# A fused attention and feed-forward kernel: the first hundred microseconds in another order

## The chip, the cores and the metric

The kernel runs on one core of a Trainium2 chip. The metric is the device time of one execution in microseconds (us). The engines are named as in the profile: PE (TensorE, matrix products), DVE (VectorE), ACT (ScalarE), POOL (GpSimd), and SP (SyncE), which here issues every DMA. Each engine takes its own instructions strictly in the order in which the program lists them, and waits at semaphores that the others raise.

## The reference

The input x is 4 batches of 2048 rows of 256 numbers, in fp32. Two layers are applied, each with a residual:

```python
x = x + layernorm(attention(layernorm(x), w_qkv, out_w, out_b))
x = x + layernorm(ffn(layernorm(x), W_r, W_k, W_v, mu_r, mu_k))

# attention: one head of width 256; rows 0-63 and 192-255 of the contraction in fp16, the rest in fp32
q, k, v = split(mixed_precision_matmul(x, w_qkv), 3)
s = softmax(q / sqrt(256) @ k.T)
y = (s @ v) @ out_w.T + out_b

# ffn: x_prev is x shifted by one row in the sequence
xr = mu_r * x + (1 - mu_r) * x_prev;  xk = mu_k * x + (1 - mu_k) * x_prev
out = sigmoid(xr @ W_r.T) * (square(relu(xk @ W_k.T)) @ W_v.T)
```

## The kernel before, in words

**Numbers.** A value that has to be exact beyond fp16 is kept as a high and a low fp16 part, and a product is the sum of three fp16 matmuls. The normed x is stored as three planes of 128 columns (`low`, `high`, and `rest`, which is what `high` leaves over), and DMA transposes turn them into `turned`. Two weight pairs are multiplied together once at the start: the query and key weights into one matrix `qk` (QK_BANK), and the value and output weights into one (FOLD_BANK). So the kernel needs only "queries" = x times `qk`, scores = queries times x, values = probabilities times x, and one projection.

**Tiling.** A batch is 4 groups of 512 rows for preparation (`n` in `pre_stats_of(n)`, `planes_low(n)`, `turn_planes(n)`; group 0 in two halves) and 8 units of 256 rows for queries (`h`, H = 32 in all). A unit has 8 score blocks of 128 x 512; block k = 8h + u is five matmuls of 512 columns into one of three PSUM banks (`scores(k)`, L1457 to L1461), and DVE copies it out and takes its maximum (`score_out(k)`, L1134). Block k waits until DVE has copied out block k - 3. In unit 0, blocks 0 and 1 read group 0 of `turned`, blocks 2 and 3 group 1, blocks 4 and 5 group 2, blocks 6 and 7 group 3.

**Slots.** Every engine has a loop over slots k = 0 ... 255. In slot k PE does score block k and then what is due there; the other engines do their shares of the units underway. The constants at the head of the file (L88 to L99 and those above) say in which slot something is due: `at(k, X)` is unit h if k = 8h + X. So queries of unit h are made in slot 8h - 6 by PE, rounded (q_hi) in slot 8h - 5 by ACT and their low part (q_lo) in slot 8h - 3 by DVE; score block 8h waits for it.

**The head.** Before the loop come, by hand, the load and rounding of the query and key weights, their transposes (L1554) and product (L1566), the scale of it (largest element, summed over partitions by the matmul L1586, `weight_factors`), then the parts of group 0, `queries(0)`, and for groups 1 to 3 the chain

- DVE `pre_stats_of` (L1010) and `pre_moments_of` (L1016), the row statistics;
- POOL `pre_rsqrt` (L513, L518), their inverse roots;
- DVE `pre_norm` (L1022);
- ACT `planes_high` (L752), POOL `planes_low` (L674), the three planes;
- SP `turn_planes` (L386), the transpose.

Between them PE runs matmuls on a constant tile whose result is not used (`keep_clock`, L1572; WARM gives their counts at four places). At the end of slot 1 PE transposes the value and output weights (`turn_weight(2)`, `(3)`), makes `queries(1)` and multiplies the two weights (`multiply_weights(2, 3, ...)`); in slot 7 it transposes the other three. Then the scales of these weights are found: peaks on DVE (slots 1 and 8), a transpose and a spreading matmul on PE (slots 15 and 19), `diagonal_of_peaks` and `tops` on DVE (slots 17 and 20), `scales` on POOL (one slot later), and the weights are rounded in two pairs by ACT (slots 24 and 27) and DVE (25 and 28). The softmax of unit 0 is spread over slots 7 to 14 (exponentials and high parts on ACT, low parts on POOL and DVE), and its values begin on PE in slot 23.

Of the kernel before, what the change touches and what calls it, by code (L numbers as in the profile page):

```python
# [18 lines left out]
def sandwich(nc, x, w_qkv, out_w, out_b, w_r, w_k, w_v, mu_r, mu_k, out):  # L19
# [3 lines left out]
    NJ = N // BLK  # L23
# [67 lines left out]
    NORM_AT = 0  # L91
    V_AT = 1
    WEIGHT_PEAKS_AT = 1
    FIRST_LOW = 2
    WARM = (22, 8, 28, 16)
    PREP, PREP_EVERY = 23, 11
    PREP_LOAD, PREP_STATS, PREP_RSQRT, PREP_NORM, PREP_HIGH, PREP_LOWER, PREP_TURN = -8, 0, 1, 2, 4, 5, 6
    WEIGHTS_AT, VAL_AT, PEAKS_AT, PEAKS_TURN_AT, DIAGONAL_AT, SPREAD_AT, TOPS_AT = 7, 9, 8, 15, 17, 19, 20
    W_HIGH_AT, W_LOW_AT = (24, 27), (25, 28)  # L99
# [11 lines left out]
    with ctx:  # L111
# [250 lines left out]
        def _(sp):  # L362
# [79 lines left out]
            load_weight(3)  # L442
            for i, m in enumerate((mu_r, mu_k)):
                for h in range(HALVES):
                    sp.dma_start(mu[:, i, h:h + 1], m[h * P:(h + 1) * P].rearrange("(p a) -> p a", a=1)).then_inc(vec_in, 16)
            turn_planes(1)
# [3 lines left out]
            reload_x(NJ)  # L450
            reload_x(NJ + 1)
            for k in range(SLOTS):
# [8 lines left out]
                if (n := prep(k, PREP_LOAD)) is not None and n >= NJ + 2:  # L461
                    reload_x(n)
# [26 lines left out]
        def _(pool):  # L489
# [190 lines left out]
            pre_rsqrt(2)  # L680
            pre_rsqrt(3)
            planes_low(1)
# [67 lines left out]
        def _(act):  # L750
# [166 lines left out]
            query_high(1)  # L917
            row_norms_of()
            for k in range(SLOTS):
# [21 lines left out]
                if (h := at(k, Q_HIGH)) is not None and h >= 2:  # L941
                    query_high(h)
# [6 lines left out]
                if k == VAL_AT:  # L949
                    keep_val()  # L950
# [56 lines left out]
        def _(dve):  # L1007
# [282 lines left out]
            dve.wait_ge(x_in[1], 16)  # L1290
            stats_of(1, range(1))
# [3 lines left out]
            stats_of(1, range(1, 2))  # L1295
            weight_factors()
            half_low(1)
            stats_of(1, half(1))
            qk_low()
            pre_moments_of(1)  # L1300
            pre_stats_of(2)
            pre_moments_of(2)
            query_low(0)
            pre_norm(1)
            pre_stats_of(3)
            pre_moments_of(3)
            pre_norm(2)
            dve.wait_ge(kappa_made, 2)
            for k in range(SLOTS):
                score_out(k)  # L1310
                if k == NORM_AT:
# [5 lines left out]
                if (h := at(k, Q_LOW)) is not None and h >= 1:  # L1317
                    query_low(h)
# [9 lines left out]
                for i in range(2):  # L1328
                    if (h := at(k, MIX[i])) is not None:
                        mix(h, i)  # L1330
                if (h := at(k, INVERT)) is not None:
# [88 lines left out]
        def _(pe):  # L1420
# [170 lines left out]
            for k in range(SLOTS):  # L1591
# [10 lines left out]
                if (h := at(k, FEED)) is not None:  # L1602
                    feed(h)
                if k == V_AT:
# [3 lines left out]
                    pe.wait_ge(q_lo_made, 1)  # L1608
                    queries(1)
                    multiply_weights(2, 3, FOLD_BANK, out_multiplied)  # L1610
                if (h := at(k, QUERY)) is not None and h >= 2:
                    pe.wait_ge(q_lo_made, h)
                    queries(h)
# [73 lines left out]
```

## Time and profile before

| | us |
|---|---|
| median of 3 runs | 810.1 (809.94 to 810.55) |
| the profiled execution, its own time | 810.1 |
| its span in the trace | 808.3 |
| PE busy | 783.5 (97%) |
| DVE busy | 655.2 (81%) |
| ACT busy | 574.8 (71%) |
| POOL busy | 516.0 (64%) |

The span runs from the first to the last record; 1.8 us of the execution lie outside it. Of the chain of waits that ended last, PE holds 91%. A busy share is an average over the whole span, so the stage that the change touches, the first 60 us, has to be read in the timelines of the engines, one beside the other.

### The profile page before, as it was taken

To read this page: it belongs to the slowest core of one execution; us is meant where nothing else is said; L and a number is where in the kernel's file an instruction comes from. 1 tells how busy PE (TensorE), PEld (TensorE's weight loads), DVE (VectorE), ACT (ScalarE), POOL (GpSimd) and SP (SyncE) were. 2 spreads that over 40 slices of the span, in tenths; PEclk is the share of its full clock that TensorE was granted. 3 is DMA by queue.
4 is the path that set the end of the run, shared out by engine and by line. 5 is a ranking of instruction groups with operands and counts; after the bars stand their busy time and mean duration, and the time that the engine had idled before them with its cause. 6 is when DMAs were issued, how large, how long until landed. Compare 5 with 4: busy or idle time off the path is not lost.

```text
span 808.3 us, 16563 instructions
## 1 busy us (share of the span) xinstructions
PE 783.5 (97%) x5839; PEld 573.9 (71%) x5839; DVE 655.2 (81%) x1685; ACT 574.8 (71%) x791; POOL 516.0 (64%) x750
## 2 busy tenths in 40 slices
PE   8899999999999999999999999999999999998983
PEld 6547767777777777777777777777777777777862
DVE  6788888877788979878788879988777788777886
ACT  3568668877677778777768687787777776675564
POOL 2351356656766868775676767876567657676674
PEclk9999999999999999999999999999999999999999
DMA  6787788577867769787767887857577765559201
GB/s 188 151 162 129 147 152 179 90 143 145 169 130 147 137 131 168 144 148 135 111 133 139 172 164 142 158 103 136 108 139 144 131 125 91 120 119 206 74 14 52
DMA packets 348243, 108.70 MB, mean 134 GB/s; under 512 B 321920, under 2 KB 347904, under 8 KB 348160
## 3 DMA queue, kind: packets, MB, share of 16 engines
q1 hardware_dynamic: 348160, 107.64, 69.0%
q8 instruction: 46, 0.75, 0.4%
q14 instruction: 37, 0.30, 0.1%
HBM read 18.75 MB, written 8.39 MB: 34 GB/s over the span
## 4 chain that ended last, share of the span: by engine, by line
PE 91%; DVE 4%; DMA 2%; issue 1%; POOL 1%; ACT 1%; SPq 0%; POOLq 0%; DVEq 0%; ACTq 0%
PE Y L1478 7%; PE Y L1482 7%; PE Y L1481 7%; PE Y L1479 7%; PE Y L1480 7%; PE S L1457 7%; PE S L1461 7%; PE S L1460 7%; PE S L1459 7%; PE S L1458 7%; PE M L1422 6%; PE M L1424 6%; PE M L1423 6%; PE M L1437 1%; PE M L1440 1%
## 5 line engine op out<-in xcount | busy, mean ns | idle before, releaser
L1134 DVE TENSOR_SCALAR_CACHE_REDUCE probs<-S 128x512 f32<-128x512 f32 x256 | 172.9, 677 | 63.5 <-PE S L1461 63.3
L820 ACT ACTIVATE probs<-probs,exp_bias,kappa 128x2048 f32<-128x2048 f32 x64 | 133.9, 2092 | 63.6 <-DVE exp_bias L1147 63.6
L1152 DVE TENSOR_TENSOR p_lo<-probs,p_hi 128x2048 f16<-128x2048 f32 x62 | 170.1, 2743 | 7.2 <-ACT p_hi L752 7.1
L1479 PE MATMUL Y<-pt_lo,planes 128*128 128x256 f16 x496 | 135.2, 273 | 0.0
L1481 PE MATMUL Y<-pt_lo,planes 128*128 128x256 f16 x496 | 135.2, 273 | 0.0
L1478 PE MATMUL Y<-pt_hi,planes 128*128 128x256 f16 x496 | 135.2, 273 | 0.0
L1480 PE MATMUL Y<-pt_hi,planes 128*128 128x256 f16 x496 | 135.2, 273 | 0.0
L1482 PE MATMUL Y<-pt_hi,planes 128*128 128x256 f16 x496 | 135.2, 273 | 0.0
L752 ACT ACTIVATE p_hi<-probs 128x2048 f16<-128x2048 f32 x64 | 121.4, 1896 | 5.3 <-DMA pt_lo<-p_lo 5.0
L1457 PE MATMUL S<-turned,q_hi 128*128 128x512 f16 x256 | 97.1, 379 | 2.4 <-DMA turned<-planes 1.4
L1461 PE MATMUL S<-turned,q_lo 128*128 128x512 f16 x256 | 97.0, 379 | 0.0
L1459 PE MATMUL S<-turned,q_hi 128*128 128x512 f16 x256 | 97.0, 379 | 0.0
L1460 PE MATMUL S<-turned,q_hi 128*128 128x512 f16 x256 | 97.0, 379 | 0.0
L1458 PE MATMUL S<-turned,q_lo 128*128 128x512 f16 x256 | 97.0, 379 | 0.0
L569 POOL TENSOR_TENSOR avar<-amv,att_eps 128x2 f32<-128x2 f32 x32 | 8.9, 278 | 116.3 <-DVE amv L1184 116.3
L665 POOL TENSOR_TENSOR gate<-gate,res 128x256 f32<-128x256 f32 x54 | 82.5, 1547 | 0.9 <-ACT gate L902 0.9
L651 POOL TENSOR_TENSOR xm_lo<-mixed,xm_hi 128x512 f16<-128x512 f32 x61 | 77.8, 1277 | 6.2 <-ACT xm_hi L752 5.9
L1479 PEld LDWEIGHTS Y<-pt_lo,planes 128*128 128x128 f16 x496 | 48.5, 98 | 30.5
L1478 PEld LDWEIGHTS Y<-pt_hi,planes 128*128 128x128 f16 x496 | 48.5, 98 | 30.5
L1209 DVE SCALAR_TENSOR_TENSOR mixed<-diff,mu,xt 128x256 f32<-128x256 f32 x128 | 64.2, 542 | 1.5 <-POOL diff L644 1.2
L601 POOL TENSOR_TENSOR gvar<-gmv,gate_eps 128x2 f32<-128x2 f32 x32 | 6.8, 212 | 86.2 <-DVE gmv L1229 86.1
L1171 DVE SCALAR_TENSOR_TENSOR att<-M,inv_sum,bias_row 128x256 f32<-128x256 f32 x64 | 28.0, 478 | 37.5 <-PE M L1424 35.9
(223 smaller groups left out, 2031.7 us busy)
## 6 DMA issues: line engine op xcount, KB each, us to landing
x_res<-in_L_attn_x SPq DMA_DIRECT2D x32, 256.0 KB, 3.7
out_x<-gate SPq DMA_DIRECT2D x32, 256.0 KB, 3.2
xs<-in_L_attn_x SPq DMA_DIRECT2D x13, 512.0 KB, 4.6
pt_hi<-p_hi SPq DMA_TRANSPOSE x62, 5.0
pt_lo<-p_lo SPq DMA_TRANSPOSE x62, 4.8
xs<-in_L_attn_x SPq DMA_DIRECT2D x2, 256.0 KB, 4.3
gate<-in_L_attn_x SPq DMA_DIRECT2D x1, 512.0 KB, 6.9
att<-in_L_attn_x SPq DMA_DIRECT2D x1, 512.0 KB, 4.3
```

Source lines behind the costliest of these rows:

```text
L1134: dve.tensor_scalar(probs[:, h % 2, t, c * BLK:(c + 1) * BLK], S[k % RING][:, :], 1.0, None, ALU.mult, ALU.max, accum_out=chunk_max[:, t, ...
L1152: dve.tensor_tensor(p_lo[:, t, :], probs[:, h % 2, t, :], p_hi[:, t, :], ALU.subtract).then_inc(p_lo_made, 1)
L1457: pe.matmul(to, q_hi[:, h % 2, 0, rows], low, start=True, stop=False)
L1458: pe.matmul(to, q_lo[:, h % 2, 0, rows], low, start=False, stop=False)
L1459: pe.matmul(to, q_hi[:, h % 2, 1, rows], high, start=False, stop=False)
L1460: pe.matmul(to, q_hi[:, h % 2, 1, rows], rest, start=False, stop=False)
L1461: pe.matmul(to, q_lo[:, h % 2, 1, rows], high, start=False, stop=True).then_inc(s_done, 1)
L1478: pe.matmul(to[:, 0, :], low, p_h, start=first, stop=False, skip_group_check=True)
L1479: pe.matmul(to[:, 0, :], low, p_l, start=False, stop=final, skip_group_check=True)
L1480: pe.matmul(to[:, 1, :], high, p_h, start=False, stop=False, skip_group_check=True)
L1481: pe.matmul(to[:, 1, :], high, p_l, start=False, stop=False, skip_group_check=True)
L1482: mm = pe.matmul(to[:, 1, :], rest, p_h, start=False, stop=final, skip_group_check=True)
```

## The change

What it does, engine by engine:

- **SP:** the transpose of group 1 is issued ahead of four small loads (mu), not behind them. The loads of x for groups 4 and 5 move from before the loop to slots 15 and 26.
- **POOL:** `planes_low(1)` stands ahead of `pre_rsqrt(3)`, not behind it.
- **ACT:** `query_high(1)` moves into slot 3, and the row norms of a weight (`row_norms_of`) move from before the loop to slot 6, with `keep_val` (from slot 9).
- **DVE:** the statistics of the first two tiles of group 1 move behind `half_low(1)` (they stood one by one in front of `weight_scale` and `weight_factors`). `query_low(0)` moves behind `pre_norm(1)`, and the moments of group 2 behind that. `pre_norm(2)` and the moments of group 3 move into slot 0, `pre_norm(3)` into slot 1, the peaks of three weights from slot 1 to slot 4. In every slot `query_low` stands behind `probs_low`, `attention`, the statistics and `mix`, not ahead of them.
- **PE:** `queries(1)` moves from slot 1 to slot 2, and the product of the value and output weights from slot 1 to slot 3; the other three transposes from slot 7 to slot 5. The unused matmuls are 22, 18, 18, 12, not 22, 8, 28, 16.
- The search for the scales and the rounding of the weights move from slots 15 ... 28 to slots 11 ... 20.

```diff
-    NORM_AT = 0
+    NORMS_AT = (0, 1)
     V_AT = 1
-    WEIGHT_PEAKS_AT = 1
+    WEIGHT_PEAKS_AT = 4
-    WARM = (22, 8, 28, 16)
+    WARM = (22, 18, 18, 12)
-    WEIGHTS_AT, VAL_AT, PEAKS_AT, PEAKS_TURN_AT, DIAGONAL_AT, SPREAD_AT, TOPS_AT = 7, 9, 8, 15, 17, 19, 20
-    W_HIGH_AT, W_LOW_AT = (24, 27), (25, 28)
+    FOLD_AT, WEIGHTS_AT, VAL_AT, PEAKS_AT, PEAKS_TURN_AT, DIAGONAL_AT, SPREAD_AT, TOPS_AT = 3, 5, 6, 8, 11, 12, 15, 16
+    W_HIGH_AT, W_LOW_AT = (17, 19), (18, 20)
@@ SP
             load_weight(3)
+            turn_planes(1)
             for i, m in enumerate((mu_r, mu_k)):
...
-            turn_planes(1)
             turn_planes(2)
             turn_planes(3)
             sp.dma_start(bias_row[:, :], ...)
-            reload_x(NJ)
-            reload_x(NJ + 1)
...
-                if (n := prep(k, PREP_LOAD)) is not None and n >= NJ + 2:
+                if (n := prep(k, PREP_LOAD)) is not None:
                     reload_x(n)
@@ POOL
             pre_rsqrt(2)
+            planes_low(1)
             pre_rsqrt(3)
-            planes_low(1)
             planes_low(2)
@@ ACT
             planes_high(3)
-            query_high(1)
-            row_norms_of()
...
-                if (h := at(k, Q_HIGH)) is not None and h >= 2:
+                if (h := at(k, Q_HIGH)) is not None and h >= 1:
                     query_high(h)
...
                 if k == VAL_AT:
+                    row_norms_of()
                     keep_val()
@@ DVE
             half_norm(0)
-            dve.wait_ge(x_in[1], 16)
-            stats_of(1, range(1))
             weight_scale()
             half_low(0)
             half_norm(1)
-            stats_of(1, range(1, 2))
             weight_factors()
             half_low(1)
+            dve.wait_ge(x_in[1], 16)
+            stats_of(1, half(0))
+            qk_low()
             stats_of(1, half(1))
-            qk_low()
             pre_moments_of(1)
             pre_stats_of(2)
+            pre_norm(1)
+            query_low(0)
             pre_moments_of(2)
-            query_low(0)
-            pre_norm(1)
             pre_stats_of(3)
-            pre_moments_of(3)
-            pre_norm(2)
             dve.wait_ge(kappa_made, 2)
             for k in range(SLOTS):
                 score_out(k)
-                if k == NORM_AT:
+                if k == NORMS_AT[0]:
+                    pre_norm(2)
+                    pre_moments_of(3)
+                if k == NORMS_AT[1]:
                     pre_norm(3)
...
-                if (h := at(k, Q_LOW)) is not None and h >= 1:
-                    query_low(h)
                 if (ht := exp_at(k, FIRST_LOWER, LOWER)) is not None and (ht[1] > 0 or ht[0] >= FIRST_LOW):
                     probs_low(*ht)
...
                         mix(h, i)
+                if (h := at(k, Q_LOW)) is not None and h >= 1:
+                    query_low(h)
@@ PE
+                if (h := at(k, QUERY)) is not None and h >= 1:
+                    pe.wait_ge(q_lo_made, h)
+                    queries(h)
                 if k == V_AT:
                     pe.wait_ge(w_rounded, 2)
                     turn_weight(2)
                     turn_weight(3)
-                    pe.wait_ge(q_lo_made, 1)
-                    queries(1)
+                if k == FOLD_AT:
                     multiply_weights(2, 3, FOLD_BANK, out_multiplied)
-                if (h := at(k, QUERY)) is not None and h >= 2:
-                    pe.wait_ge(q_lo_made, h)
-                    queries(h)
```

## Rows read from the trace of the kernel before

**Rows 1.** Page, part 1: busy us, share of the span, instructions per engine.
```profile
PE 783.5 (97%) x5839; PEld 573.9 (71%) x5839; DVE 655.2 (81%) x1685; ACT 574.8 (71%) x791; POOL 516.0 (64%) x750
```

**Rows 2.** Windows: length, busy us (instructions) per engine, clock, DMA share, GB/s.
```profile
17.90:26.77 8.87, 6.50 (x36) 4.12 (x37) 8.72 (x23) 6.00 (x13) 4.30 (x6) 1.00 0.75 187
...
45.27:57.00 11.73, 10.74 (x60) 5.55 (x59) 9.90 (x32) 8.45 (x7) 5.32 (x5) 1.00 0.76 143
57.00:120.00 63.00, 63.00 (x451) 44.03 (x452) 54.33 (x144) 41.71 (x53) 24.31 (x50) 1.00 0.80 146
```

**Rows 3.** Timeline of PE: start, us, what, [idle before <- releaser].
```profile
11.00 0.38 PE L1586 MATMUL M<-w_peak,twos 128*128 128x1 f32 x2
...
17.90 0.38 PE L1457 MATMUL S<-turned,q_hi 128*128 128x512 f16 x1 [0.38 <-DMA turned<-planes]
...
21.31 0.65 PE L1554 MATMUL Y<-ident,pt_hi 128*128 128x128 f32 x4 [1.09 <-ACT pt_hi L752]
...
23.74 1.99 PE L1566 MATMUL M<-res 128*128 128x256 f32 x8 [0.24 <-ACT res L752]
26.77 0.39 PE L1457 MATMUL S<-turned,q_hi 128*128 128x512 f16 x1 [1.04 <-DMA turned<-planes]
...
27.86 0.38 PE L1457 MATMUL S<-turned,q_hi 128*128 128x512 f16 x1
...
37.81 0.27 PE L1437 MATMUL M<-turned,qk_hi 128*128 128x256 f16 x1
...
38.90 0.38 PE L1457 MATMUL S<-turned,q_hi 128*128 128x512 f16 x1
...
46.50 0.39 PE L1457 MATMUL S<-turned,q_hi 128*128 128x512 f16 x1 [0.86 <-DVE probs L1134]
```

**Rows 4.** Timeline of DVE.
```profile
12.18 0.14 DVE L1074 TENSOR_SCALAR w_sum<-M 128x1 f32<-128x1 f32 x1
...
14.37 0.37 DVE L1016 BATCH_NORM_AGGREGATE pmv<-pst 128x2 f32<-128x6 f32 x4
14.66 1.37 DVE L1010 BATCH_NORM_STATS2 pst<-gate 128x6 f32<-128x256 f32 x4
...
16.47 0.66 DVE L1125 SCALAR_TENSOR_TENSOR q_lo<-M,q_hi 128x512 f16<-128x512 f32 x1
17.05 1.37 DVE L1022 TENSOR_SCALAR xs<-xs,pmv,prstd 128x256 f32<-128x256 f32 x4
...
43.55 2.28 DVE L1152 TENSOR_TENSOR p_lo<-probs,p_hi 128x2048 f16<-128x2048 f32 x1
...
53.77 1.93 DVE L1120 TENSOR_SCALAR weight_scale_of<-inv_top 128x4 f32<-128x4 f32 x1
```

**Rows 5.** Timeline of POOL.
```profile
15.10 1.01 POOL L518 TENSOR_TENSOR prstd<-pvar,minus_half 128x4 f32<-128x4 f32 x1
...
21.72 1.16 POOL L674 TENSOR_TENSOR planes<-xs,planes 128x512 f16<-128x512 f32 x1
...
51.60 4.08 POOL L670 TENSOR_TENSOR p_lo<-probs,p_hi 128x2048 f16<-128x2048 f32 x1 [9.62 <-ACT p_hi L752]
```

**Rows 6.** Timeline of ACT.
```profile
18.46 1.15 ACT L752 ACTIVATE planes<-xs 128x512 f16<-128x512 f32 x2 [2.05 <-DVE xs L1022]
...
60.81 2.10 ACT L820 ACTIVATE probs<-probs,exp_bias,kappa 128x2048 f32<-128x2048 f32 x1 [4.59 <-DVE exp_bias L1147]
...
62.90 0.67 ACT L777 ACTIVATE wt_hi<-Y,weight_scale_of 128x512 f16<-128x512 f32 x1
```

**Rows 7.** Chain that ended last: start, us, what; the transpose before score block 2.
```profile
22.90 3.82 DMA turned<-planes
```

**Rows 8.** Timeline of PE near the end.
```profile
739.35 0.28 PE L1422 MATMUL M<-wt_hi,xm_hi 128*128 128x256 f16 x1 [2.60 <-POOL xm_lo L651]
```

**Rows 9.** Windows of PE there: length, busy us (matmuls), clock, DMA share, GB/s.
```profile
740.00:741.00 1.00, 1.00 (x7) 0.50 1.21 208
...
743.00:744.00 1.00, 1.00 (x10) 0.81 1.16 220
```

## The prediction

> **What bounds the kernel.** The first part of the page comes first: PE is busy for 783.5 of the 808.3 us [rows 1]. So it is not a question of how much the other engines do but of where PE stands still, and the second view is the windows. After 57 us PE has no idle time (63.00 of 63.00 us [rows 2]), and nothing that the change touches lies later than slot 28, so the head decides. There PE is idle for 2.37 us between 17.90 and 26.77, and for 0.99 us between 45.27 and 57.00 [rows 2]. The timeline of PE names the places: block 0 waits for a transpose until 17.90, the weight transposes wait for ACT until 21.31, block 2 waits 1.04 us for the transpose of group 1 until 26.77, and the block at 46.50 waits 0.86 us for DVE [rows 3]. The point to see is that the wait before 26.77 is what is left after PE has filled the time with useful work: the two weight transposes, `queries(1)` and the weight product (1.99 us, from 23.74 [rows 3]) all lie before it. The third view is the chain and the timelines of DVE, POOL and ACT, which show what makes the transpose of group 1 late.
>
> **The change, first stretch: up to block 2.** I follow the new order on DVE with the old durations.
>
> 1. The scale of `qk`. The peak matmul now follows 18 unused matmuls, not 8. The ten extra ones cost about 0.11 us each (a 256-column fp16 matmul: the ten of `queries` take 38.90 - 37.81 = 1.09 us [rows 3]), so it moves from 11.00 to 12.1, and with its 0.38 us DVE can go on at 12.5, not at 12.18 [rows 3, 4]: +0.3 us.
> 2. Two of the four statistics of group 1 used to run in front of such waits. They are now in the open: half of 1.37 us less overlap, +0.66 [rows 4]. With 0.1 for a drain that `qk_low` covered, the moments of group 1 move from 14.37 to 15.5.
> 3. The statistics of group 2 follow at 15.8 (before: 14.66) and end at 17.1. POOL's inverse roots came 0.73 + 1.01 us behind the start of the moments (16.11 against 14.37 [rows 4, 5]), so now at 17.25. `pre_norm(1)` runs 17.3 to 18.6. It was at 17.05, so ACT's planes of group 1 (18.46 [rows 6]) hardly move: 18.6 to 19.75.
> 4. `query_low(0)` now waits in line behind `pre_norm(1)`: 18.6 to 19.3, where it started at 16.47 [rows 4]. Block 0 needs it. It starts at 19.3, not at 17.90 [rows 3]. Blocks 0 and 1 and the weight transposes are done by 22.4 instead of 22.2, so this alone costs little.
> 5. The moments of group 2 run behind it, 19.2 to 19.6. POOL makes the roots of group 2 (another 1.35 us with its gaps) before `planes_low(1)`, which starts at 21.05 instead of 21.72 and takes 1.16 [rows 5]. SP is free: the four small loads are behind the transpose now. The transpose is issued at 22.25, not at 22.90, and lands after the same 3.82 us [rows 7], at 26.1. The two edits aimed at the transpose therefore bring 0.65 us; the rest of what they could bring is eaten by steps 1 to 4.
>
> So block 2 starts at 26.1, 0.65 us earlier. But `queries(1)` (1.09 us) and the product (1.99 us alone, 1.85 in a stream) have moved behind it, and PE has nothing to do from 22.4 to 26.1. Sum: -0.65 + 1.09 + 1.85 = **+2.3 us**. Nothing later gives this back, since PE was never idle between 26.77 and 45. The transposes of groups 2 and 3 are late too, and are hidden: `pre_norm(2)` at 21.5 puts group 2 on its way at about 26.4 and group 3 at about 30.2. They land by 30.3 and 34.1, and PE comes to blocks 4 and 6 at 31.2 and 34.6 (blocks of 1.09 us [rows 3], the other three weight transposes included). The margin of the second is 0.5 us. The loads of x moved to slots 15 and 26 are first read from slot 23 on, so they are free.
>
> **The clock.** Half rate is seen in this trace where PE had stood idle for 2.60 us before 739.35 [rows 8]: the granted clock is 0.50 (1.2 GHz) in the next windows, 7 matmuls in 1 us, and on its way back to full (2.4 GHz) at 743 [rows 9]. About 3.4 us at half rate lost 1.7 us. The gaps of 1.09 and 1.04 us in the head lost nothing. The new gap, 3.7 us, is longer than 2.60, and another of almost 2 us (from the end of the 12 unused matmuls to 19.3) stands before it. The fall is the likelier outcome. Its price lies between 0 (no fall, or all of it inside the gap) and 1.7 us; part of the slow stretch may lie in the gap, and I take **+1.2 us**. The Trainium skill, TensorE: Matmul & The Clock Gate, section "HAM oscillation — how this bites in real kernels", says that a wait for a DMA between two bursts of matmuls makes the engine go back to half rate. By that rule the fall is certain here and the sum includes it; rows 8 and 9 agree with the rule, the 1 us gaps set it a lower bound.
>
> **Second stretch: slots 8 to 28.** Old: the stall of 0.86 us at 46.50, because DVE makes a low part of 2.28 us (43.55 [rows 4]) in front of two copies. New: in slot 13 `query_low(2)` stands behind that low part, and block 16 needs it. From the end of block 13: copy 0.6, low part 2.2, `query_low` 0.65, with two hand-overs 3.55 us, against 2.0 for blocks 14 and 15. Block 16 was not held before; block 17 was: 46.50 is 4.2 us after block 13's end (the low part starts 1.25 us behind that end). It now starts at 3.55 + 1.09 = 4.65: +0.45. The spreading matmul (about 0.4 with its gap) moves into this stall: -0.4. The transpose of the peaks (0.11) leaves it: +0.1. In `tops` a 128x4 operation takes 1.93 us and ends exactly with POOL's low part (51.60 + 4.08 = 55.68) [rows 4, 5]; in slot 16 POOL is idle, which takes away the rest of the old idle time, -0.1 to -0.3. Against it, ACT gets four weight roundings of 0.6 us (62.90) in slots 17 and 19, where before they stood behind a 4.59 us gap (60.81) [rows 6]. They push exponentials and the high part of slot 21 back by 2.5 us, and the low part on DVE in slot 22 behind them; block 26 would wait 0.6. Sum +0.4; the bounds are -0.9 (all idle time of this stretch gone) and +1.5 (both new waits in full, no credit). I take **+0.4 us**.
>
> `query_low` behind `mix` in later units: slot 8h - 3 holds neither `probs_low` nor `mix` from unit 3 on (their slots are 3 and 6, 0 and 2 modulo 8), so there the order is the same.
>
> **Sum.** 2.3 + 1.2 + 0.4 = 3.9 us. The profiled execution has a span of 808.3 us and a time of 810.1, which is the median of the runs, so the forecast is 812.2 in the span and **814.0 us** as time.
>
> **The rivals.**
>
> - *No fall of the clock.* Everything as above, but the slow stretch does not come. For it: gaps of 1 us cost nothing. Against: the 2.60 us gap did [rows 8, 9]. 814.0 - 1.2 = 812.8.
> - *Later still.* The transposes of groups 2 and 3 eat their margin, for DVE's norms run beside POOL's low parts and SP has four loads between transposes 1 and 2. If group 3 lands 1.5 us later than I say, block 6 waits 1.0; with the full 1.7 for the clock, 815.5.
> - *Not slower: the transpose comes as early as its inputs allow.* The place is `planes_low(1)`. If it starts right behind ACT's planes (19.75) and not behind POOL's roots of group 2, the transpose is issued at 20.95 and lands at 24.8: -1.97 + 2.94 = +0.97. The gap is then near 2.3 us and the clock holds. If the second stretch also loses its whole 0.99 us of idle time and gains a little beside, the end is 0.0: 810.1, 809.5 at best. It decides at the issue of that transpose, at about 21 us. Against it: POOL's order has `pre_rsqrt(2)` ahead, and DVE gives it its moments only behind `query_low(0)`.
> - *The delay on DVE does not come* (block 0 starts near 18 because the added overlap loss is smaller than I count), while `queries(1)` and the product still cost 2.94: the transpose about 1 us earlier, no fall: 811.4. For it: my step 2 rests on waits that were partly cover. Against: the order of `query_low(0)` is plain in the program.
>
> **How the numbers follow.** Chances: forecast 0.48, no fall 0.22, later still 0.08, not slower 0.09, no delay on DVE 0.13. A measurement of this kernel can tell about 0.2%, 1.6 us, from no change: 808.5 to 811.7. The forecast and the first two rivals lie above that, 0.78; I take 0.03 from "no fall" for a low end of its second stretch and add 0.04 of the last rival, whose 811.4 is close to the bound: slower 0.79. Within lie the other 0.09 of the last rival, that 0.03, and 0.03 of "not slower": 0.15. The other 0.06 of "not slower" I give to faster, for a case in which the second stretch brings more than its idle time. The range goes from the last rival with a little room, 811.0, to the second with a little room, 815.6.
>
> **What would show it.** In the new trace: block 0 starts near 19.3, released by q_lo; PE idle for more than 3 us before block 2, which starts near 26 and is released by `turned`; `queries(1)` and the product behind it; block 8 starts about 2.3 us later than before where the clock is full; a window of clock 0.50 within 30 us; block 16 released by q_lo in slot 16. Wrong would be: block 2 before 25, block 0 at 18, or PE idle again removed later, after 57 us, where I see none to remove.

## The result, and the profile after

The changed kernel is slower: 814.76 us in the median of 4 runs (814.14 to 815.58) against 810.02 us; the ratio is 1.0060, 95% interval 1.0043 to 1.0079. The forecast was 814.0. The profiled execution has a span of 814.2 us and a time of its own of 815.95, which is 1.2 us above the median; its stages are read below, and they add up to more than the medians differ.

The first line of the page: PE does the same work in a longer span [rows 1].

```profile
PE 784.2 (96%) x5835; PEld 574.4 (71%) x5835; DVE 655.9 (81%) x1685; ACT 574.8 (71%) x791; POOL 512.9 (63%) x750
```

The timeline of PE with the places where it waits (start, us, what, [idle before <- releaser]). The row of 25.55 stands where 26.77 stood before, 49.56 in the neighbourhood of 46.50 [rows 3].

```profile
18.84 0.39 PE L1454 MATMUL S<-turned,q_hi 128*128 128x512 f16 x1 [2.00 <-DVE q_lo L1122]
...
25.55 0.61 PE L1454 MATMUL S<-turned,q_hi 128*128 128x512 f16 x1 [3.50 <-DMA turned<-planes]
...
27.65 0.42 PE L1434 MATMUL M<-turned,qk_hi 128*128 128x256 f16 x1
...
30.11 1.89 PE L1563 MATMUL M<-res 128*128 128x256 f32 x8
31.84 0.38 PE L1454 MATMUL S<-turned,q_hi 128*128 128x512 f16 x1
...
37.47 0.38 PE L1454 MATMUL S<-turned,q_hi 128*128 128x512 f16 x1
...
49.56 0.39 PE L1454 MATMUL S<-turned,q_hi 128*128 128x512 f16 x1 [1.79 <-DVE q_lo L1122]
...
62.63 0.39 PE L1454 MATMUL S<-turned,q_hi 128*128 128x512 f16 x1 [2.07 <-DVE q_lo L1122]
```

Three things are to be seen. The waits have moved: 2.00 us before block 0 (0.38 before the change), 3.50 before block 2, and two new ones for q_lo, 1.79 before block 16 and 2.07 before block 24. The queries (27.65) and the product (30.11) now stand behind block 2. And the first matmuls of block 2 are longer than 0.39 us.

The windows of PE around that place (length, busy us and matmuls, granted clock, DMA share, GB/s):

```profile
24.00:26.00 2.00, 0.45 (x2) 0.71 0.48 73
26.00:28.00 2.00, 2.00 (x7) 0.50 0.70 120
28.00:30.00 2.00, 2.00 (x15) 0.94 0.42 77
```

The clock falls to 0.50 (1.2 GHz) between 24 and 26 us, inside the gap, and comes back between 28 and 30.

DVE and POOL in the same stretch:

```profile
15.01 0.38 DVE L1013 BATCH_NORM_AGGREGATE pmv<-pst 128x2 f32<-128x6 f32 x4
...
16.80 1.38 DVE L1019 TENSOR_SCALAR xs<-xs,pmv,prstd 128x256 f32<-128x256 f32 x4
18.10 0.68 DVE L1122 SCALAR_TENSOR_TENSOR q_lo<-M,q_hi 128x512 f16<-128x512 f32 x1
...
45.19 0.91 DVE L1107 TENSOR_SCALAR peak_diag<-ident,peak_of 7x7 f32<-7x7 f32 x1
...
57.44 0.75 DVE L1087 SCALAR_TENSOR_TENSOR wt_lo<-M,weight_scale_of,wt_hi 128x512 f16<-128x512 f32 x1 [0.37 <-ACT wt_hi L775]
58.10 3.25 DVE L1087 SCALAR_TENSOR_TENSOR wt_lo<-relu,weight_scale_of,wt_hi 128x512 f16<-128x512 f32 x1
...
61.89 0.08 DVE L1131 DVE_READ_ACCUMULATOR probs<-S 128x1 f32 x1
```

```profile
20.41 1.16 POOL L672 TENSOR_TENSOR planes<-xs,planes 128x512 f16<-128x512 f32 x1
...
41.99 4.09 POOL L668 TENSOR_TENSOR p_lo<-probs,p_hi 128x2048 f16<-128x2048 f32 x1 [12.99 <-ACT p_hi L750]
...
56.73 4.08 POOL L668 TENSOR_TENSOR p_lo<-probs,p_hi 128x2048 f16<-128x2048 f32 x1
```

SP issues the transpose of group 1 at 21.59 and not at 22.90 [rows 7], and it lands 3.9 us later:

```profile
21.59 1.45 SPq L386 DMA_TRANSPOSE turned<-planes  x1
```

Where the time went, by the start of a score block in the two profiled executions (the last column names what was added or gained since the row above):

| start of | before | after | difference | what added |
|---|---|---|---|---|
| block 2 | 26.77 | 25.55 | -1.2 | earlier transpose |
| block 8 | 34.57 | 37.47 | +2.9 | product and queries +2.8, half rate +1.3 |
| block 17 | 46.50 | 50.65 | +4.15 | order of q_lo and a held operation +0.65, a later q_hi from ACT +0.6 |
| block 24 | 56.97 | 62.63 | +5.7 | a held rounding: +1.5 |
| block 28 | 66.75 | 72.41 | +5.7 | |
| end | 808.3 | 814.2 | +5.9 | |

Nothing is added between blocks 24 and 28, and 0.2 us in all that follows. In this pair of executions the whole loss is made in 63 us. The parts of block 17's row, and what "held" means, follow with the experiments.

### The profile page after: what moved, and what is told of

It reads as the page before. It is cut to its first block, busy times and chain, and to the rows that moved or that the text cites. A ratio compares the mean times of both kernels' runs of the same rounds, so it can differ in the third digit from the quotient of the medians.

```text
span 814.2 us, 16555 instructions
## 1 busy us (share of the span) xinstructions
PE 784.2 (96%) x5835; PEld 574.4 (71%) x5835; DVE 655.9 (81%) x1685; ACT 574.8 (71%) x791; POOL 512.9 (63%) x750
## 4 chain that ended last, share of the span: by engine, by line
PE 90%; DVE 4%; DMA 2%; issue 1%; ACT 1%; POOL 1%; SPq 0%; POOLq 0%; DVEq 0%; ACTq 0%
PE Y L1475 7%; PE Y L1479 7%; PE Y L1477 7%; PE Y L1478 7%; PE Y L1476 7%; PE S L1454 6%; PE S L1458 6%; PE S L1455 6%; PE S L1457 6%; PE S L1456 6%; PE M L1419 6%; PE M L1421 6%; PE M L1420 6%; PE M L1434 1%; PE M L1435 1%
## 5 line engine op out<-in xcount | busy, mean ns | idle before, releaser
L567 POOL TENSOR_TENSOR avar<-amv,att_eps 128x2 f32<-128x2 f32 x32 | 6.8, 211 | 116.3 <-DVE amv L1181 116.3
```

## The experiments

Each is given with its edit, what was expected before it ran, and what came. Times are medians. The kernel before was run again beside each of three groups of experiments, with 810.03, 810.12 and 810.08 us. Where a start of a block or a length of a stretch is given, it is that of the one profiled execution.

### The order of query_low in the slots undone

```diff
+                if (h := at(k, Q_LOW)) is not None and h >= 1:
+                    query_low(h)
                 if (ht := exp_at(k, FIRST_LOWER, LOWER)) is not None and (...):
                     probs_low(*ht)
...
-                if (h := at(k, Q_LOW)) is not None and h >= 1:
-                    query_low(h)
```

> The changed kernel with query_low ahead of probs_low in each slot of DVE, as before the change. Theory: block 16 no longer waits for q_lo at the far side of the 2.3 us low part (1.79 us of wait); block 17 then waits for its bank as in the kernel before (about 1.2 us), so block 17 starts 0.5 us earlier. Whether the end follows depends on the wait at block 24: if that is set by POOL's low part (fixed by ACT and the scales, which also move up by 0.5), the end is 0.5 us earlier, 814.3. Rival: the order costs the whole 1.79 us and the kernel is 1.8 us faster, 813.0.

Measured: 814.77 us (812.95 to 816.9), ratio to before 1.0060 (1.0039 to 1.0081); the median is that of the changed kernel. The timeline of PE:

```profile
51.24 0.39 PE L1454 MATMUL S<-turned,q_hi 128*128 128x512 f16 x1 [1.20 <-DVE probs L1131]
...
63.73 0.49 PE L1454 MATMUL S<-turned,q_hi 128*128 128x512 f16 x1 [2.57 <-DVE q_lo L1122]
```

The wait before block 16 is gone, and block 17 waits 1.20 us for its bank instead. From block 8 to block 17 this kernel takes 12.7 us (38.55 to 51.24) and the changed one 13.2: the half microsecond of the theory. It did not reach the end: the wait before block 24 grew from 2.07 to 2.57, because POOL's low part (57.8 to 61.9 here) did not move against block 8. These rows refute the rival; the times alone, which scatter over 4 us, would not. The profiled execution is the slowest of the four (816.9): its clock was at 0.50 once more from 63.9 to 67.3, behind that wait, where the changed kernel kept 1.00.

### The second rounding of weights two slots later

```diff
-    W_HIGH_AT, W_LOW_AT = (17, 19), (18, 20)
+    W_HIGH_AT, W_LOW_AT = (17, 19), (18, 22)
```

> The changed kernel with the second pair of low weight parts on DVE in slot 22 (behind the low part of the probabilities there), not in slot 20. The same work, at a time when POOL's low part (56.7 to 60.8) is over. Theory 'lock' (the DVE operation of 3.25 us was held by POOL's operation on the same memory port): both roundings take 0.75 us, block 24 no longer waits for q_lo (2.07 us before), and the kernel is 1.5 to 2.1 us faster, about 813.0. Rival 'load' (DVE simply has 1.4 us more to do in these slots): the rounding takes 3 us here too or another operation does, block 26 waits instead, and the gain is under 0.5 us.

Measured: 813.87 us (812.82 to 814.3), ratio 1.0043 (1.0027 to 1.0060), 0.9 us better than the changed kernel. DVE and PE in this kernel:

```profile
64.05 0.74 DVE L1087 SCALAR_TENSOR_TENSOR wt_lo<-relu,weight_scale_of,wt_hi 128x512 f16<-128x512 f32 x1
```

```profile
65.45 0.39 PE L1454 MATMUL S<-turned,q_hi 128*128 128x512 f16 x1 [1.30 <-DVE probs L1131]
```

The rounding of the last weight takes 0.74 us here and took 3.25 in the changed kernel, with the same operands. Block 24 no longer waits, so the mechanism "lock" holds. Of the "load" rival the duration is refuted, but the wait of block 26 that it named is there: it waits for a copy that stands behind the low part on DVE (61.18 to 63.47) and behind the two roundings themselves, 1.3 us of work in their new slot. So only part of the 2.07 us came through; from block 17 to block 28 it takes 21.0 us, not 21.8. The size of 1.5 to 2.1 was wrong, measured 0.9.

### The whole second stretch as before the change

```diff
-    ... PEAKS_TURN_AT, DIAGONAL_AT, SPREAD_AT, TOPS_AT = ..., 11, 12, 15, 16
-    W_HIGH_AT, W_LOW_AT = (17, 19), (18, 20)
+    ... PEAKS_TURN_AT, DIAGONAL_AT, SPREAD_AT, TOPS_AT = ..., 15, 17, 19, 20
+    W_HIGH_AT, W_LOW_AT = (24, 27), (25, 28)
     (and query_low ahead of probs_low, as above)
```

> The changed kernel with the second stretch of the kernel before: query_low ahead of probs_low, and the search for the scales and the rounding of the weights in slots 15 to 20 and 24 to 28. What is left of the change is the first stretch. Theory: block 8 stays 2.9 us late (1.6 for the moved queries and product less the earlier transpose, 1.3 for the clock), the waits at blocks 16 and 24 shrink to the 0.9 us of the kernel before, and the kernel is 2.5 to 2.8 us faster than the changed one and 2.0 to 2.9 slower than before: about 812.2. Rival (the second stretch hides lateness of the first): it comes back to within 1 us of the kernel before.

Measured: 812.27 us (810.96 to 812.99), ratio 1.0027 (1.0015 to 1.0039). Its PE rows:

```profile
25.24 0.48 PE L1454 MATMUL S<-turned,q_hi 128*128 128x512 f16 x1 [3.29 <-DMA turned<-planes]
...
50.07 0.39 PE L1454 MATMUL S<-turned,q_hi 128*128 128x512 f16 x1 [1.46 <-DVE probs L1131]
```

By the medians, undoing the second stretch gives back 2.5 of the 4.7 us and leaves 2.2. The rows divide otherwise. Block 8 is 3.0 us later than before (37.53) and block 28 3.6 us later (70.33). From block 8 to block 28 the kernel before takes 32.18 us, the changed one 34.94 and this one 32.80: 2.1 us are undone and 0.6 are left. That this execution still ends only 1.9 us behind the kernel before comes from the clock near the end. At the wait of 2.6 us there, where the clock of the kernel before fell [rows 8, 9], it did not fall here, and from block 28 to the end this kernel takes 739.9 us and not 741.6:

```profile
743.00:745.00 2.00, 2.00 (x20) 1.00 1.15 219
```

So the agreement with the expected 812.2 is partly luck. The 0.6 us that are left lie before block 17 (1.46 us of waiting, before the change 0.86). They come from ACT. The first exponential of unit 0 started 0.87 us before block 8 and now starts 0.32 us after it, for the other three weight transposes, which stood between blocks 7 and 8, stand in slot 5 now, and block 8 follows block 7 at once. Then q_hi is late and DVE waits for it. The first row is from the kernel before, the other two are from this one:

```profile
33.70 2.09 ACT L820 ACTIVATE probs<-probs,exp_bias,kappa 128x2048 f32<-128x2048 f32 x1 [6.40 <-DVE exp_bias L1147]
...
37.85 2.09 ACT L818 ACTIVATE probs<-probs,exp_bias,kappa 128x2048 f32<-128x2048 f32 x1 [1.68 <-DVE exp_bias L1144]
...
46.52 0.69 DVE L1122 SCALAR_TENSOR_TENSOR q_lo<-M,q_hi 128x512 f16<-128x512 f32 x1 [0.52 <-ACT q_hi L750]
```

No run moved these transposes alone; all nine profiled kernels that have them in slot 5 start this exponential 0.3 us after block 8, and all five that have them in slot 7 start it 0.9 to 1.0 us before.

### The moved queries and product alone, in the kernel before

```diff
                     turn_weight(3)
-                    pe.wait_ge(q_lo_made, 1)
-                    queries(1)
+                if k == 3:
                     multiply_weights(2, 3, FOLD_BANK, out_multiplied)
-                if (h := at(k, QUERY)) is not None and h >= 2:
+                if (h := at(k, QUERY)) is not None and h >= 1:
```

> The kernel before with one part of the change: on PE the queries of unit 1 in slot 2 and the product of the value and output weights in slot 3, both behind the wait for the transpose of group 1 and no longer in front of it. Theory 'fill': block 2 starts at 26.8 as before, PE is idle for over 4 us in front of it, block 8 is 1.1 + 1.75 = 2.8 us later plus about 1.3 for the half-rate stretch: 3 to 4 us slower than before, 813 to 814.2. Rival: later waits absorb it, under 1 us.

Measured: 815.15 us (813.08 to 815.92), ratio 1.0061 (1.0044 to 1.0078). This one part costs as much as the whole change. Its row of block 2 in the timeline of PE, and the windows behind it:

```profile
27.13 0.39 PE L1457 MATMUL S<-turned,q_hi 128*128 128x512 f16 x1 [4.20 <-DMA turned<-planes]
```

```profile
28.00:30.00 2.00, 2.00 (x10) 0.50 0.78 146
30.00:32.00 2.00, 2.00 (x9) 0.66 0.68 135
```

The gap is 4.20 us, the clock falls behind its end, and block 8 starts at 39.42, 4.85 us later than before: 0.36 from a later start of the stretch, 2.8 the moved work and 1.7 the half rate.

### The gap before block 2 filled

```diff
                     turn_weight(3)
+                    keep_clock(32)
```

> The changed kernel with 32 unused 256-column matmuls on PE behind the weight transposes of slot 1, so that PE is busy (about 3.5 us) until the transpose of group 1 lands. Theory 'clock' (the gap before block 2 costs its own length, and besides it a stretch at half rate worth 1.3 us): block 2 starts where it did (about 25.5), the granted clock stays at 1.00 between 24 and 30 us, and the kernel is 1.3 us faster than the changed kernel, about 813.4. Rival 'phase' (the half-rate stretch would have come at this place anyway or its cost is absorbed by later waits): within 0.3 us of the changed kernel, 814.8.

Measured: 818.52 us (818.02 to 819.35), ratio 1.0106: 3.8 us slower than the changed kernel, against both theories. The windows of PE show a first reason; a row of DVE and one of POOL are shown for the lock:

```profile
20.00:22.00 2.00, 2.00 (x6) 0.50 0.65 211
22.00:24.00 2.00, 2.00 (x14) 0.68 0.65 123
```

```profile
59.50 2.28 DVE L1087 SCALAR_TENSOR_TENSOR wt_lo<-relu,weight_scale_of,wt_hi 128x512 f16<-128x512 f32 x1
```

```profile
57.14 4.09 POOL L668 TENSOR_TENSOR p_lo<-probs,p_hi 128x2048 f16<-128x2048 f32 x1
```

The half rate came at 20 us, behind the 2.00 us gap before block 0, and the filling itself ran in it, so that block 2 starts at 27.13 and not at 25.55. A second half-rate stretch lies at 50.6 to 54.0 us. Up to block 28 (72.84) only 0.4 us are lost against the changed kernel; 1.5 more come near the end, with a wait that the next experiment shows. The profiled execution (818.02) is the fastest of the four, so that the rest of the 3.8 us is not in this trace. (The rounding on DVE takes 2.28 us here, not 3.25: it began later beside a POOL operation that ends at 61.23, and ended 0.55 after it.)

### Both gaps filled

```diff
-    WARM = (22, 18, 18, 12)
+    WARM = (22, 18, 18, 28)
...
                     turn_weight(3)
+                    keep_clock(28)
```

> The changed kernel with unused matmuls in both gaps of the first stretch: 28, not 12, behind queries(0) (the gap of 2.0 us before block 0) and 28 behind the weight transposes of slot 1 (the gap of 3.5 us before block 2). The first try filled the second gap alone, and the half-rate stretch then began in the first, under the filling. Theory 'clock': with both filled, the clock is 1.00 from the start to block 16, blocks 0 and 2 start where they did, block 8 is 1.3 us earlier than in the profiled execution of the changed kernel, and the median falls by the price times the share of executions in which the clock fell, about 1 us: 813.8. Rival: filling costs as much as it saves (block 2 is pushed back): 814.8 or more.

Measured: 816.80 us (815.47 to 817.32), ratio 1.0086. In the head it went as the theory says:

```profile
19.36 0.39 PE L1454 MATMUL S<-turned,q_hi 128*128 128x512 f16 x1 [0.26 <-DVE q_lo L1122]
...
25.90 0.39 PE L1454 MATMUL S<-turned,q_hi 128*128 128x512 f16 x1 [0.21 <-DMA turned<-planes]
...
746.55 0.28 PE L1419 MATMUL M<-wt_hi,xm_hi 128*128 128x256 f16 x1 [3.42 <-POOL xm_lo L649]
```

The waits are 0.26 and 0.21 us, the clock is 1.00 until block 24, and blocks 2 to 8 take 10.61 us, not 11.92. The end is nevertheless 2 us later than without filling (in the profiled executions 1.4). Two parts are to be seen. First, the clock fell behind the wait of 2.07 us before block 24, at 61.7 to 65.1, where the changed kernel had the same wait and kept 1.00: blocks 24 to 28 take 11.46 us, not 9.78. So the saving of 1.3 us before block 8 is lost again 25 us later. Second, near the end PE waits 3.42 us for POOL's xm_lo, where the kernel before waits 2.60 [rows 8] and the changed one 2.61. In all four kernels with added unused matmuls this wait is 3.4 to 4.5 us; in the ten other profiled executions of this case it is 2.6.

In the chain that leads to that wait ACT's high part waits for the landing of a transpose of a low part. The first row is from the changed kernel, the second from this one; the last is this one's DMA queue of instruction loads in the window 735.5 to 736.5 us (packets, MB, share of 16 engines):

```profile
732.98 5.09 DMA pt_lo<-p_lo
...
733.66 5.94 DMA pt_lo<-p_lo
...
q8 instruction: 1, 0.02, 5.5%
```

This transpose takes 5.1 to 5.2 us in the ten executions and 5.9 to 7.0 in the four, and the wait grows by just as much in each. In the four a load of 16 KB of instructions falls into its flight, in the ten none does: there the load comes after the landing, in the flight of the next such transpose, which takes 5.6 to 5.9 us there and 4.4 in the four. This queue loads once for about every 254 of PE's matmuls and weight loads (46 times for twice 5835), so matmuls added in the head move every later load against the work. Over all 14 traces the transposes of high and low parts of probabilities take 5.7 us in the median with one of these loads in their first 4 us (352 of them) and 4.8 without (1384). No run moved a load alone, so this is what fits all 14 traces, not what an experiment has shown.

### The same filling with the second stretch of before

```diff
     (the second stretch as before the change, and:)
+    WARM = (22, 18, 18, 28)
+                    keep_clock(28)
```

> The changed kernel with the second stretch of the kernel before (query_low in front, scales and weight rounding in slots 15 to 28) and with both gaps filled as in the run above. If lateness is the sum of three terms (moved queries and product less the earlier transpose 1.6 us; half rate about 1; second stretch 2.5), only the first is left: 1.2 to 1.8 us slower than before, 811.6. Rival: there is a further term that I have not seen, and it stays above 812.3.

Measured: 813.31 us (812.44 to 815.14), ratio 1.0050 (1.0036 to 1.0063), 1 us slower than without the filling. Block 28 starts at 69.21, 2.5 us after the kernel before, 1.1 us earlier than unfilled; the wait near the end is 3.6 us, 1.0 longer, and behind it the clock fell (743.3 to 746.8), where the unfilled execution kept it. The rival is right: there were further terms, these two, and the 0.6 us of the later q_hi.

### The moved work alone, with its gap filled

```diff
     (queries(1) and the product moved, in the kernel before, and in their place:)
                     turn_weight(3)
+                    keep_clock(34)
```

> The kernel before with queries(1) and the product moved behind the wait for the transpose of group 1, as in the run that moved only these two, and with 34 unused matmuls where they were. PE does as much as in that run, with no gap in front of block 2. Theory: the clock holds, and what is left is the bare length of the moved work, 2.8 us: 812.9, and 2 us faster than the run without the filling. Rival: the length of the moved work was not the price, and it stays at 815.

Measured: 815.28 us (814.69 to 815.84), ratio 1.0069. The head again does what was said: block 8 at 37.21, 2.6 us later than before, where the kernel without the filling was 4.85 later. The time does not follow: the wait near the end is 4.45 us, 1.85 longer than before. So the head supports "fill", and the time alone would refute it.

### query_low(0) ahead of pre_norm(1)

```diff
             pre_stats_of(2)
-            pre_norm(1)
             query_low(0)
+            pre_norm(1)
```

> The changed kernel with query_low(0) ahead of pre_norm(1). Theory: block 0 starts 1.3 us earlier (near 17.6), but block 2 still waits for the transpose of group 1, so PE only waits at another place: within 0.4 us of the changed kernel, apart from the clock. Rival (the late block 0 is on the path): 1.3 us faster, 813.4.

Measured: 817.51 us (816.46 to 817.86), ratio 1.0095.

```profile
17.58 0.38 PE L1454 MATMUL S<-turned,q_hi 128*128 128x512 f16 x1 [0.78 <-DMA turned<-planes]
...
25.09 0.55 PE L1454 MATMUL S<-turned,q_hi 128*128 128x512 f16 x1 [3.48 <-DMA turned<-planes]
```

Block 0 starts 1.3 us earlier, as said, and block 2 still waits 3.48 us for the same transpose. So the late block 0 is not on the path, and the rival is refuted. That the median is 2.7 us higher was not expected. In the profile block 8 is where it was (37.38), but a second half-rate stretch (62 to 66 us, behind the 2.07 us wait) makes blocks 24 to 28 1.6 us later. The profiled execution (816.46) shows that, and it is the fastest of the four; the other three were not profiled, so that the rest of the 2.7 us stays open.

### The low plane of group 1 still earlier on POOL

```diff
             pre_rsqrt(1)
-            pre_rsqrt(2)
             planes_low(1)
+            pre_rsqrt(2)
             pre_rsqrt(3)
```

> The changed kernel with the low plane of group 1 ahead of the roots of group 2 too. It is the point from which my rival 'not slower' was to decide. Theory: the low plane starts at 19.3, the transpose is issued at 20.5 and lands at 24.4, block 2 starts 1.1 us earlier; the gap before it shrinks to 2.4 us, and if the clock then holds, 1.3 more: 1.1 to 2.4 us faster, 812.4 to 813.7. Rival: group 2 is late by 0.9 us and takes it back, 814.7.

Measured: 815.89 us (815.21 to 818.48), ratio 1.0080 (1.0061 to 1.0098), 1.1 us slower by the medians, with an interval that overlaps that of the changed kernel: no gain, where 1.1 to 2.4 us were expected. SP and PE:

```profile
21.07 1.76 SPq L386 DMA_TRANSPOSE turned<-planes  x1
...
19.28 0.39 PE L1454 MATMUL S<-turned,q_hi 128*128 128x512 f16 x1 [2.00 <-DVE q_lo L1122]
...
26.10 0.39 PE L1454 MATMUL S<-turned,q_hi 128*128 128x512 f16 x1 [1.93 <-DMA turned<-planes]
```

The transpose is issued 1.0 us earlier against its stage (21.07; the stage starts 0.44 later here), but it lands 5.0 us after its issue, not 3.9 as in the changed kernel, so block 2 gains nothing. The last of the four weight loads was issued at 18.98, 2.1 us before it; in the changed kernel it was 3.9 us before. The clock fell behind the 2.0 us gap at 19.28, again behind 26.10, and a third time at 51.3. This was the point from which the rival "not slower" was to decide. In this execution the earlier issue is lost in the later landing. Why it lands later no run tells; the last weight load lands at 23.4 here and at 23.3 in the changed kernel, in the middle of the transpose in both.

### The same idea in the kernel before

```diff
-            pre_rsqrt(3)
             planes_low(1)
+            pre_rsqrt(3)
```

> The kernel before with one part of the change: on POOL the low plane of group 1 ahead of the roots of group 3. Theory: its transpose is issued at 21.4 (when SP has issued the four small loads) and not at 22.9, lands at 25.2, and the 1.04 us of idle time before block 2 disappear, since PE is busy until 25.7 anyway: 1.0 us faster, 809.0. Rival 'next in line': group 2 or 3 is late instead, gain under 0.3.

Measured: 809.57 us (808.24 to 810.18, 11 runs), ratio 0.9992 (0.9983 to 1.0000).

```profile
24.03 1.99 PE L1566 MATMUL M<-res 128*128 128x256 f32 x8 [1.10 <-ACT res L752]
...
30.73 0.39 PE L1457 MATMUL S<-turned,q_hi 128*128 128x512 f16 x1 [0.26 <-DMA turned<-planes]
```

Block 2 starts at 25.86 with no wait, 0.9 us earlier. Half of it is given back: the product waits 1.10 us for ACT and block 6 waits 0.26 for its transpose; block 28 is 0.35 us earlier. The gain is half of what was expected, 0.55 us of 1.0, and the interval of the ratio just reaches 1.

### That, and the low part of unit 0 a slot later

```diff
     (planes_low(1) ahead of pre_rsqrt(3), as above, and:)
-    FIRST_LOWER = (10, 13)
+    FIRST_LOWER = (10, 14)
```

> The kernel before with the low plane of group 1 ahead of the roots of group 3 on POOL (measured alone: 0.5 us faster), and the low part of the second half of unit 0 on DVE one slot later (14, not 13), so that block 17 does not wait for a copy behind it. Theory: the 0.86 us wait before block 17 goes, block 18 waits 0.4 instead: 0.4 us faster than the first edit alone, 809.1. Rival: the wait moves on in full, 809.6.

Measured: 809.91 us (808.88 to 812.31, 11 runs), ratio 1.0004 (0.9995 to 1.0012): no faster than before.

```profile
53.22 2.41 DVE L1120 TENSOR_SCALAR weight_scale_of<-inv_top 128x4 f32<-128x4 f32 x1
...
51.52 4.08 POOL L670 TENSOR_TENSOR p_lo<-probs,p_hi 128x2048 f16<-128x2048 f32 x1 [9.75 <-ACT p_hi L752]
...
47.03 0.39 PE L1457 MATMUL S<-turned,q_hi 128*128 128x512 f16 x1 [0.39 <-DVE probs L1134]
...
56.90 0.39 PE L1457 MATMUL S<-turned,q_hi 128*128 128x512 f16 x1 [0.62 <-DVE q_lo L1125]
```

Block 17 starts at 45.40, 0.74 us earlier than with the first edit alone, and the wait before block 18 is the 0.39 foreseen. The 809.1 that was expected did not come, nor did the first edit's gain. It is lost again: in slot 20 an operation on 4 numbers per row waits 2.41 us for POOL's low part (51.52 + 4.08 = 55.60; 53.22 + 2.41 = 55.63), q_lo is late and block 24 waits. No version beats the kernel before clearly.

## Why the prediction was right

Three terms were summed: 2.3 us for the first stretch, 1.2 for the clock, 0.4 for the second. The profiled execution has 1.6, 1.3 and 2.8, and 0.2 after that, 5.9 in all. The first term was 0.7 too large, the third 2.4 too small, and the median lies 1.2 us under the profiled execution. The mechanism of the first two is right; that the forecast came within 0.8 us of the median is in part luck.

**First stretch, steps 1 to 5.** Right in order and cause. The moments of group 1 ran at 15.01 (said: 15.5), `pre_norm(1)` at 16.80 (17.3), block 0 at 18.84 (19.3), the transpose was issued at 21.59 (22.25) and block 2 started at 25.55 (26.1), 3.50 us of waiting (3.7). All times are some 0.5 us too late in my account, 0.3 us of it because this execution reached the product of `qk` earlier (7.90 against 8.22), the rest from step 1. The stretch without the clock came to +1.6, or +1.9 without that head start, not +2.3. The experiments confirm what sets it: block 2 waits for the transpose whatever happens to block 0, and the moved 2.8 us are the price.

**The clock.** Right in size where it happens. Blocks 2 to 8 take 11.9 to 12.3 us in six profiled kernels in which the clock fell there (the changed kernel and those with the order undone, the old second stretch, the moved work alone, query_low(0) first, the low plane earlier) and 10.6 in the others with this order of work: 1.3 to 1.7 us. It does not always happen. The kernel with the later rounding had the same gap, 3.48 us, and kept 1.00; the kernel with the low plane earlier fell behind gaps of 2.0. The Trainium skill, TensorE: Matmul & The Clock Gate, section "HAM oscillation — how this bites in real kernels", says that such a wait between bursts brings the engine back to half rate. These traces agree at six of the seven unfilled gaps before block 2 and not at that one. The prediction counted the fall as certain by the rule and likely by the rows; the rows were the better guide, and they were weaker than the prediction took them. The wait of 2.6 us near the end, on which they rest [rows 8, 9], stands in ten profiled executions, and the clock fell there in five of them: from block 28 to the end those take 741.6 to 741.7 us and the others 739.9 to 740.9.

**Second stretch.** The mechanism was half right and the size wrong: +0.4 was said (the terms listed there add up to 0.45 to 0.65), +2.8 measured between blocks 8 and 28 of the profile; undoing the stretch took 2.1 of it away there, and 2.5 us off the median. Block 16 waited for q_lo behind the low part, as said. What failed first is the step that costed operations at their free duration in their new slots. I had seen one operation of DVE end exactly with POOL's low part [rows 4, 5], and booked only the relief. The new slots put two others under the same fate. `peak_diag` (7 numbers a row) ran 0.91 us beside the low part of 41.99 + 4.09 = 46.08, where it took 0.22 before (row below); with the old order of q_lo it is worth at most 0.15 us (the kernel with the order undone takes 12.7 us from block 8 to 17, the one with the whole old second stretch 12.54). The rounding from relu at 58.10 ran 3.25 us and ended 0.54 after 56.73 + 4.08 = 60.81. In five more kernels it ended 0.54 or 0.55 after POOL as well, with durations of 2.2 to 3.27 us. The rounding just before it, of the same size but from PSUM (57.44), took 0.75 beside the same operation. So it is the rounding with both its tensors in SBUF that is held.

```profile
48.95 0.22 DVE L1110 TENSOR_SCALAR peak_diag<-ident,peak_of 7x7 f32<-7x7 f32 x1
```

The Trainium skill, SBUF — State Buffer, section "Who interferes with whom", states it: a DVE instruction with two SBUF inputs contends with a GpSimd instruction that reads SBUF. One with at most one such input does not, outside the modes in which DVE uses two ports for one tensor; `tensor_scalar` can enter these. For the two roundings these traces agree, with 3.25 and 0.75 us. `peak_diag` and the 128x4 operation are `tensor_scalar` with one tensor in SBUF and were held too; whether they ran in such a mode no view shows.

The second step that failed is one that the prediction does not have: it moved the three weight transposes to slot 5 and put the effect on ACT at nothing. It is the +0.6 us of the later q_hi.

**ACT's four roundings.** Said to delay block 26 by 0.6. In the changed kernel it does not wait. With the rounding two slots later DVE waits 2.67 us for ACT's high part and starts its low part 1.5 us into block 24, where the others start it 0.5 us in: the delay by ACT is there. The 1.3 us that block 26 waits are not its price, for the two roundings on DVE, 1.3 us of work, stand there in front of the same copy. What ACT's delay costs alone is not shown.

**The rivals.** "No fall" is what the profiled execution with the later rounding did before block 2; the profiled one of the changed kernel fell, and its other runs were not profiled. "Not slower" was tried at its own point and failed on the landing of the transpose. "The delay on DVE does not come" is refuted: block 0 started at 18.84, released by q_lo (and its 811.4 should have been 811.8, 814.0 less 1.2 for the clock and 1 for the transpose). "Later still" (transposes of groups 2 and 3) did not occur: blocks 4 and 6 never waited. After 57 us nothing of the old idle time was there to be removed, but the second stretch added to it up to block 24.

**What stays open.** The median (+4.7) is 1.2 us less than the profiled difference; the profiled execution is the slowest of the five, and the places where the clock falls vary between executions. How the other four divide is not known. That an instruction load is what lengthens the wait near the end fits every trace but was not tried by itself.

## What to carry to other kernels

Work that stands in front of a wait is free up to the length of that wait; before moving it behind, read what is left of the wait: 2.8 us of matmuls moved behind a transfer that came 1.2 us earlier cost more than they could bring, and left a gap in which the clock could fall. An operation has its short duration only in the slot where it was measured: before moving it, look at what POOL does in the new slot if it is one of DVE. Filling a gap for the clock's sake has to be judged by the whole time, since here it won up to 1.7 us at its place and the kernels ended 0 to 4 us later: the next wait let the clock fall instead, and more instructions on PE moved the loads of its program into other transfers. And a median of some executions is not the sum of one trace: list where the clock was low in both traces before dividing a difference among causes.

## What the runs showed of the hardware

- A 7x7 operation of DVE took 0.91 us and a 128x4 one 2.41 us beside a 4.08 us operation of POOL, each ending within 0.03 us of it; without it they took 0.22 and 0.17.
- A 128x512 rounding of DVE with both tensors in SBUF took 2.2 to 3.3 us beside such an operation and ended 0.54 or 0.55 us after it, in six kernels; with one of them in PSUM it took 0.75 beside the same operation.
- The granted clock fell behind idle times of 1.9 to 2.1 us in several executions (in the kernel with the low plane still earlier on POOL, twice in 10 us), and did not fall behind one of 3.48 us. Behind the same wait of 2.6 us it fell in five executions of ten. One stretch at half rate cost 1.3 to 1.7 us between blocks 2 and 8 and 1.7 between blocks 24 and 28.
- The transpose that sets the wait near the end landed after 5.1 to 5.2 us in ten executions and after 5.9 to 7.0 in the four in which 16 KB of instructions were loaded during its flight.
- A transpose issued 2.1 us after the last of four weight loads landed after 5.0 us; issued 3.9 us after it, it landed after 3.9 (one execution each).
